# Decoder layer on one core: the second row's query work placed inside the first row's softmax, half of the first row's weighing on DVE, and the FFN squares placed ahead of the third weighing

## What is computed

```
x = layernorm(x + mamba(x))                      # first pass of the kernel
q = x @ Wq.T + bq;  k = ctx @ Wk.T + bk;  v = ctx @ Wv.T + bv      # 77 context tokens, 16 heads of 32
s = where(masked, -inf, q @ k.T / sqrt(32));  p = softmax(s)
x = layernorm(x + (p @ v) @ Wo.T + bo)           # second pass
xr, xk = mu * x + (1 - mu) * (x one token earlier)                 # two mixes, mu_r and mu_k
x = layernorm(x + sigmoid(xr @ Wr.T) * (square(relu(xk @ Wk.T)) @ Wv.T))   # second pass
```

## Time and profile before

| | |
|---|---|
| three timed runs | 2473.32, 2486.76, 2489.14 us; median 2486.76 |
| the profiled execution | 2481.5 us, its span 2479.7 us |
| PE busy | 2328.2 us (94% of the span) |
| DVE, ACT, POOL busy | 1837.8, 1564.3, 1675.1 us |
| mean granted TensorE clock | 0.983 of full |

### The profile page before, as it was taken

How to read it: one execution, slowest core, us unless ns; L and a number is a source line. 1 busy time by engine, 2 the same in 40 slices (tenths; PEclk the granted TensorE clock), 3 DMA queues, 4 the chain that set the end, 5 groups by cost and what they waited for, 6 DMA issues and landing times. The chain is left out here.

```text
span 2479.7 us, 38405 instructions
## 1 busy us (share of the span) xinstructions
PE 2328.2 (94%) x15232; PEld 1387.1 (56%) x15232; DVE 1837.8 (74%) x2164; ACT 1564.3 (63%) x2604; POOL 1675.1 (68%) x911
## 2 busy tenths in 40 slices
PE   8888999999999999999999998997799999999998
PEld 4565666566565666556666655564445554554543
DVE  4998898898899899889889887772465466366463
ACT  4786787878778788778787887751433443333332
POOL 1898899898899889889989988882333233143130
PEclk9999999999999999999999999999899999999999
DMA  6677878887877888787887787876000110000000
GB/s 206 140 154 162 217 158 177 219 171 163 211 161 172 186 196 178 157 223 162 177 218 171 165 219 154 192 159 211 28 28 7 35 35 1 34 18 1 18 17 17
DMA packets 103525, 329.57 MB, mean 133 GB/s; under 512 B 9571, under 2 KB 46819, under 8 KB 72627
## 3 DMA queue, kind: packets, MB, share of 16 engines
q0 software_dynamic: 27648, 201.34, 41.3%
q1 hardware_dynamic: 75699, 125.78, 14.9%
HBM read 107.25 MB, written 18.51 MB: 51 GB/s over the span
## 5 line engine op out<-in xcount | busy, mean ns | idle before, releaser
L1020 POOL TENSOR_TENSOR mamba_ring<-mamba_ring,mamba_c_row 128x1024 f32<-128x1024 f32 x512 | 1277.7, 2652 | 45.2 <-DVE mamba_ring L908 44.3
L908 DVE TENSOR_TENSOR_SCAN mamba_ring<-mamba_ring,ps 128x512 f32<-128x512 f32 x1024 | 1175.1, 1201 | 142.6 <-PE ps L452 136.9
L713 ACT ACTIVATE mamba_ring<-mamba_delta,mamba_a_neg 128x512 f32<-128x512 f32 x1024 | 659.7, 710 | 79.0 <-DMA mamba_ring<-mamba_ring 77.7
L452 PEld LDWEIGHTS ps<-shared,mamba_v_t 64*128 64x128 f32 x8192 | 499.4, 189 | 249.3 <-issue 149.7
L452 PE MATMUL ps<-shared,mamba_v_t 64*128 64x128 f32 x8192 | 581.1, 284 | 53.8 <-DVE mamba_ring L908 52.8
L1029 POOL DMA_DIRECT2D mamba_ring<-mamba_ring x192 | 181.0, 943 | 147.2 <-DMA mamba_ring<-mamba_ring 117.2
L1674 POOL TENSOR_TENSOR xf_pr<-xf_pr,xf_top 128x1232 f32<-128x1232 f32 x32 | 75.0, 2343 | 256.6 <-DVE xf_top L1577 256.6
L418 PE MATMUL ps<-mamba_xt,mamba_wres 128*128 128x512 f32 x512 | 242.4, 617 | 0.0
L361 PE MATMUL ps<-mamba_xt,mamba_wu 128*128 128x512 f32 x464 | 218.5, 615 | 5.6 <-DMA mamba_xt<-x_t 5.6
L882 DVE SCALAR_TENSOR_TENSOR mamba_u<-ps,mamba_wcv,mamba_u 128x511 f32<-128x511 f32 (+2 forms) x192 | 142.1, 740 | 73.5 <-ACT mamba_u L678 71.0
L504 PE MATMUL ps<-mamba_wout,mamba_u 128*128 128x512 f32 x352 | 168.0, 611 | 0.0
(11 more groups left out here) (149 smaller groups left out, 2842.4 us busy)
## 6 DMA issues: line engine op xcount, KB each, us to landing
mamba_ring<-mamba_ring POOLq DMA_DIRECT2D x192, 1024.0 KB, 7.8
mamba_c_row<-c_rows SPq DMA_DIRECT2D x32, 1024.0 KB, 11.4
mamba_wres<-w_res SPq DMA_DIRECT2D x64, 256.0 KB, 6.1
mamba_wu<-w_u SPq DMA_DIRECT2D x58, 256.0 KB, 4.1
x_rows<-x SPq DMA_DIRECT2D x32, 256.0 KB, 9.0
mamba_xt<-x_t SPq DMA_DIRECT2D x7, 1024.0 KB, 10.6
x<-x_rows SPq DMA_DIRECT2D x28, 256.0 KB, 5.0
xf_xn<-x SPq DMA_DIRECT2D x16, 256.0 KB, 7.9
```

Of the source, the lines that this page charges most:

```text
L452: m = nc.tensor.matmul(ps[:, 2 * s + i, tb * P:(tb + 1) * P], v_t[g % 2][i * H:(i + 1) * H, tb * P:(tb + 1) * P], diag_b[i * H:(i + 1) * H ...
L713: a = nc.scalar.activation(ring[:, q % NR, i, :], delta[:, d % EARLY, :], ACT.Exp, scale=a_neg[:, d, 2 * k + i:2 * k + i + 1])
L908: m = nc.vector.tensor_tensor_scan(ring[:, r, i, :], ring[:, r, i, :], both[:, bass.ds(i, T, 2)], 0.0, ALU.mult, ALU.add)
L1020: nc.gpsimd.tensor_tensor(ring[:, q % NR], ring[:, q % NR], c_row[:, 2 * k:2 * k + 2, :], ALU.mult).then_inc(c_done, 1)
```

## The change

Three edits, all in the second pass. No arithmetic is added or taken away.

1. Row 1's four x transposes and its q products 0 and 1 move from behind row 0's attention into row 0's softmax: the transposes stand between scores 2 and 3 of row 0, the two q products behind scores 3. Their copies on ACT (`front_x(1)`, `take_q(1, 0)`, `take_q(1, 1)`) stand between row 0's exponentials. In row 1, q products 2 and 3 now stand ahead of `x2_transposes(0)` instead of behind it, and nothing of row 1's q work is left behind it. POOL's `prepare(1)` now waits for the end of row 0's attention products.
2. In row 0 alone, the weighing of tiles 2 and 3 is done by DVE (`weigh_first`) instead of POOL.
3. In rows 1 to 7, POOL's `squares(b - 1, (2, 3))` stands ahead of `weigh(b, 2)` instead of behind it.

```diff
@@ sequence numbers of the PSUM banks
     def front_a(b):
-        return 0 if b == 0 else b * ROW_A - FFN
+        return 0 if b == 0 else FRONT if b == 1 else b * ROW_A - FFN
...
     def attend_a(b):
-        return b * ROW_A + FRONT
+        return b * ROW_A + FRONT + (KT + 2 if b == 0 else 0)
@@ PE, attend(b)
-                if b + 1 < NB:
+                if 0 < b < NB - 1:
                     x1_transposes(b + 1)
@@ PE, row(b)
-                q_product(b, 0)
-                q_product(b, 1)
-                if b > 0:
+                if b != 1:
+                    q_product(b, 0)
+                    q_product(b, 1)
+                if b > 1:
                     x2_transposes(b - 1)
                 q_product(b, 2)
                 q_product(b, 3)
+                if b == 1:
+                    x2_transposes(0)
...
                     for tb in range(TT):
                         scores(b, tb)
+                        if tb == 2:
+                            x1_transposes(1)
+                    q_product(1, 0)
+                    q_product(1, 1)
                     pe.wait_ge(w_loaded, 16 * len(loads))
@@ ACT, row(b)
                 for tb in range(TT):
                     exp(b, tb)
+                    if b == 0 and tb == 1:
+                        front_x(1)
+                    if b == 0 and tb >= 2:
+                        take_q(1, tb - 2)
@@ DVE
+            def weigh_first(tb):
+                dve.wait_ge(shares, tb * 3 + 3)
+                nc.vector.tensor_tensor(pr[:, tb], pr[:, tb], total[:, tb].unsqueeze(2).broadcast_to([P, NH, NK]),
+                                        ALU.mult).then_inc(probs, 1)
...
+                    if tb == 3 and first:
+                        weigh_first(2)
                 dve.wait_ge(topped, b * TT + TT)
                 shares_of(b, TT - 1)
+                if first:
+                    weigh_first(TT - 1)
@@ POOL, prepare(b)
-                pool.wait_ge(a_filled, front_a(b) + KT)
+                pool.wait_ge(a_filled, attend_a(0) + ATTEND if b == 1 else front_a(b) + KT)
@@ POOL, row b
                 centre(b, 3)
-                weigh(b, 2)
                 if b > 0:
                     squares(b - 1, (2, 3))
-                weigh(b, 3)
+                    weigh(b, 2)
+                    weigh(b, 3)
```

More of the change, by code:

```diff
@@ L1066, in front_a @@
     def front_a(b):
-        return 0 if b == 0 else b * ROW_A - FFN
+        return 0 if b == 0 else FRONT if b == 1 else b * ROW_A - FFN
     def q_a(b, j):
+        if b == 1:
+            return front_a(1) + KT + j + (ATTEND if j >= 2 else 0)
         return front_a(b) + KT + j + (KT if b > 0 and j >= 2 else 0)
     def x2_a(b):
-        return LAST_A if b == NB - 1 else front_a(b + 1) + KT + 2
+        return LAST_A if b == NB - 1 else ROW_A - FFN + FRONT if b == 0 else front_a(b + 1) + KT + 2
     def ffn_a(b):
-        return LAST_A if b == NB - 1 else front_a(b + 1) + FRONT
+        return LAST_A if b == NB - 1 else (b + 1) * ROW_A - FFN + FRONT
     def attend_a(b):
-        return b * ROW_A + FRONT
+        return b * ROW_A + FRONT + (KT + 2 if b == 0 else 0)
     def scores_v(b):
@@ L1321, in values @@
                         h = j * HB + i
-                        m = nc.tensor.matmul(ps[i * DK:(i + 1) * DK, n % 4, :], v_cur[0:NK, h * DK:(h + 1) * DK],
+                        m = nc.tensor.matmul(ps[i * DK:(i + 1) * DK, (a + n) % 4, :], v_cur[0:NK, h * DK:(h + 1) * DK],
                                              pt[0:NK, h % (2 * HB), :], start=True, stop=True,
@@ L1336, in attend @@
                         for tb in range(TT):
-                            m = nc.tensor.transpose(ps[0:NK, n % 4, tb * P:(tb + 1) * P], pr[:, tb, h, :], ident[:])
+                            m = nc.tensor.transpose(ps[0:NK, (a + n) % 4, tb * P:(tb + 1) * P], pr[:, tb, h, :], ident[:])
                         m.then_inc(a_filled, 1)
@@ L1462, in values @@
                     act.wait_ge(a_filled, a + (n + 1))
-                    nc.scalar.copy(ot[:, j, :], ps[:, n % 4, :]).then_inc(a_taken, 1)
+                    nc.scalar.copy(ot[:, j, :], ps[:, (a + n) % 4, :]).then_inc(a_taken, 1)
                 for j in range(KT):
@@ L1468, in attend @@
                         act.wait_ge(a_filled, a + (n + 1))
-                        nc.scalar.copy(pt[0:NK, h % (2 * HB), :], ps[0:NK, n % 4, :]).then_inc(a_taken, 1)
+                        nc.scalar.copy(pt[0:NK, h % (2 * HB), :], ps[0:NK, (a + n) % 4, :]).then_inc(a_taken, 1)
                         n += 1
@@ L1483, in row @@
             def row(b):
-                front_x(b)
+                if b != 1:
+                    front_x(b)
                 if b == 0:
@@ L1491, in row @@
                     rstd_of(z2_stats, 2 * TT, mv, rstd, rstd2_ln, rstd2, b - 1)
-                take_q(b, 0)
-                take_q(b, 1)
+                if b != 1:
+                    take_q(b, 0)
+                    take_q(b, 1)
+                else:
+                    take_q(b, 2)
+                    take_q(b, 3)
                 if b > 0:
@@ L1496, in row @@
                     scale_x2(b - 1, xk, muk, range(KT))
-                take_q(b, 2)
+                if b != 1:
+                    take_q(b, 2)
                 if b > 0:
                     scale_x2(b - 1, xr, mur, (0, 1))
-                take_q(b, 3)
+                if b != 1:
+                    take_q(b, 3)
                 if b > 0:
```

## The result

| | before | after |
|---|---|---|
| timed | 2481.02 us (median of 8, 2473.32 to 2489.14) | 2464.3 us (median of 8, 2454.8 to 2475.47) |
| ratio | | 0.994, 95% interval 0.9921 to 0.996 |
| the profiled execution, its span | 2481.5, 2479.7 us | 2475.5, 2473.7 us |
| the second pass in it (from the first transposes to the end) | 769.6 us | 755.3 us |

The medians are 16.7 us apart; the forecast was 2468 and 16.4 less. The ratio by itself makes 14.9 us of 2481. Its interval holds neither no change nor a gain of 1%.

The account below looks back on a forecast made before the run. PE, busy 94% of the span, was taken as the bound. 0.5 + 1.80 + 6.87 - 2.63 + 9.9 = 16.4 us less than the middle of four times gave 2467.7, forecast as 2468, range 2455 to 2482.

Parts of the forecast that it names:

- Part 1, the transposes: Row 1's x transposes, moved between row 0's scores 2 and 3: gain 1.80 us, cost nothing.
- Part 2, the q products: Row 1's q products 0 and 1, moved behind row 0's scores 3: gain 6.87 us, cost 0.
- upper end of 1.5 us: Cost of the moved q products if wholly at half clock: they end 1.5 us after the weighing is done.
- Part 3, the bare chain: Row 1's x2 chain, no longer covered: `ffn_k` starts 4.38 us after the x2 transposes, PE waits, cost 2.63 us.
- Part 4, the weighing: Row 0's tiles 2 and 3 on DVE: 1.44 us per product, bounds 1.44 and 2.25, gain 0.5 us.
- Part 5, the squares: POOL's squares earlier in 7 rows: the 1.41 us wait ahead of `ffn_v` goes, gain 9.9 us, lower end 8.0.
- The clock in `attend(0)`: Row 0's first heads: half clock kept after a gap of about 5 us, term 0, between gain 1.9 and loss 0.9.
- The clock in row 1: Gap of 2.63 us ahead of row 1's first `ffn_k` product: clock taken as kept, no loss.
- The rival with 0.28: Clock falls in row 1's new gap, losing about 3 us: gain 13.4, time 2470.7; chance 0.28.
- the squares are what `ffn_v` waited for: At `ffn_v`; the rival denied it, saying freed banks might hold it: gain 6.5 us, time 2477.6; chance 0.06.
- The late input: Rival at row 1's moved transposes: input lands late and row 0's attention queues behind it, ending slower; chance 0.02.
- the turning point: Row 1's input must land by 1737.7; each microsecond beyond costs one, and the gain is gone at 1754.1.

Follow-up runs that it names:

- e1: Kernel before with the third edit alone, POOL's squares ahead of the weighing of tile 2 in rows 1 to 7; 2469.33 us, 0.9954 of before.
- e3: Kernel before with the second edit alone, row 0's tiles 2 and 3 weighed by DVE; one time, 2473.14 us, beside a median before of 2480.88.
- e8: Kernel before with row 1's input loaded after the FFN weights and row 2's input; one time, 2474.8 us.
- e12: Kernel before with the third edit alone (the squares), run again in more rounds; 2468.2 us, 0.9967 of before.
- e2: Kernel before with the first edit alone, row 1's x transposes and q products 0 and 1 in row 0's softmax; 2467.16 us, 0.9942 of before.
- e4: The changed kernel as it is, timed again beside the single edits on the same chip; 2465.31 us, 0.9936 of before.
- e7: Changed kernel with row 1's input loaded after the three FFN weights and row 2's input; one time, 2463.67 us.
- e10: The changed kernel as it is, a third time, on the same chip as e9; 2465.2 us, 0.9949 of before.
- e11: Kernel before with the first edit alone (the moved transposes and q products), run again in more rounds; 2471.77 us, 0.9978 of before.
- e6: Changed kernel with products whose result is overwritten put in PE's three gaps (row 0, row 1, last block); 2458.69 us, 0.9916 of before.
- e5: Changed kernel with a third q product of row 1 moved into row 0's softmax; one time, 2452.89 us.
- e9: Changed kernel with a third q product moved and overwritten products in the three gaps left in row 1 and the last block; 2458.02 us, 0.9913 of before.

## Why the prediction was right, point by point

The time (2464.3) and the gain (16.7 us for 16.4) came out as forecast. By its steps:

- *Part 1, the transposes:* right. From the heads' start to the output product it fell from 15.42 us (mean of before, e1, e3, e8, e12) to 13.75 (mean of after, e2, e4, e7, e10, e11), with the clock's differences in both. Take the column "heads" off, in which those lie, and it is 9.40 in each of the five and 7.60 in each of the six, to 0.01: 1.80, as forecast. In their new place they took 3.67 us, at half clock as expected (3.5), and the start of the heads didn't move (26.67 in e2 as in e1).
- *Part 2, the q products:* right, and cost nothing. The clock was back for both of them (7.13 us for 16 passes, at other places 7.03), so the upper end of 1.5 us was not touched.
- *Part 3, the bare chain:* right to the hundredth in its start (4.38 us), so 4.24 of 6.87 us stayed; the trace has 4.14, as the x2 transposes start 0.1 us later behind the output product (20.70 for 20.60).
- *Part 4, the weighing:* right. 1.44 us for each product; 0.5 us at the heads. The bound of 2.25 wasn't needed.
- *Part 5, the squares:* right, and 60% of the gain. 1.41 us in each row, in every profile with the edit, and in none without it.
- *The clock in `attend(0)`:* half clock at its start, as taken. The two profiles differ by 0.9 us (heads 6.51 for 5.58), but that is the draw of the execution: with the gap of 13 us the heads took 5.58 to 6.34 us, 6.02 in the mean of five, and with that of 6 us 5.12 to 6.51 (e7's gap of 3.7 taken in), 6.14 in the mean of six. The term of 0 was right. The new gap was given as "about 5 us (1749.2 to 1755.0)", which is 5.8; it is 6.15.
- *The clock in row 1:* this is the step that failed. "The new gap of 2.63 us in row 1 is shorter than the one that lowered the clock; I take it as kept." It fell in 5 of 6 profiles with that gap, which measures 2.46 us (after, e2, e7, e10, e11; not in e4). The rival with 0.28 was the usual case. Its price was over-sized, though: 5.29 - 3.53 = 1.76 us, not 3, because the clock was back before the first product had ended. So the sum that the traces bear out is 16.4 - 1.8 = 14.6 us, and the traces have 15.4 (the changed kernel's own three differ by 2.7). That the medians came within 0.3 us of 16.4 is therefore luck: the ratio of the same measurement makes 14.9, and e10 found 12.9. The forecast of 2468 was 3.7 too high, of which 3.1 is the kernel before, taken at 2484.1 and measured at 2481.0.

The Trainium skill's page "TensorE: Matmul & The Clock Gate", section "HAM oscillation — how this bites in real kernels", tells of a kernel whose clock is throttled again in the wait for a DMA between two bursts of products, so that the next burst starts cold; its waits, about 3 to 5 us by the page, are longer than the gap here. The traces agree for this shorter gap too, in 5 of 6 cases. e6 shows that work in the gap takes the loss away.

- *Rivals:* the squares are what `ffn_v` waited for (e1). The late input is real as a mechanism, as e7 shows; the turning point was given as 1.5 us after PE gets there and was 2.5, since scores 3 need 1.2 to 1.4 us behind the transposes and not the 3.13 that I had taken. The prediction put those 3.13 down to the clock alone. With DVE still freeing the banks, scores took 2.27 us at full clock and 3.14 at half; with the banks free and a full clock they take 1.13. So 1.1 us of it was the banks, which are free behind the transposes, and 0.9 the clock, which was back in time.

What stays open: why the two edits' timings of the first chip, of five and four runs, were both too good. The untouched first pass ended anywhere between 1699.3 and 1718.4 us, and a median of four or five has that in it. The traces show what goes with it: over the 14 profiles the time for which the clock was at half within the first pass runs from 38 us (e5, 1699.3) to 65 us (after, 1718.4), and the longer passes are those with more of it (correlation 0.90). That doesn't say which is the cause, as the waits differ too (PE waited 52.8 us for DVE at L452 in before, 61.0 in after), and no run here separates the two.

## What to carry to other kernels

Take the path apart by what ends last at each point: a piece of work moved into a gap is worth its length only until the next chain is bare (two q products gave 4.1 of 6.9 us, the third at most 0.33 of 3.4). The smallest edit gave the most: putting two instructions that the bound engine waits for ahead of one that nobody waits for yet, in a loop body that repeats seven times (9.7 of the 15.4 us in the traces). And when you make work earlier, count what it depends on again: the load of row 1's input had 36.6 us to spare and has 5.3 now. When an untouched part of a program varies by more than the gain, compare stretches of the trace that begin where all engines have met, not whole spans.

## What the hardware showed that I had not expected

- A gap of 2.46 us in PE's work lowered the clock in 5 of 6 executions, while one of 2.71 us (e5, e9, ahead of the heads) left it full in both. So the length of a gap alone doesn't tell. What does, the runs don't separate. The fall comes up to a microsecond behind the gap, inside the work that follows, and cost 1.8 us.
- Products whose result is thrown away paid: 22 passes of 0.43 us each in gaps (e6) took 3.8 to 6.5 us off the stretch to the end (729.75 for 733.6 to 736.2), and every wait ended where it had ended without them.
